# A decoder layer on one core: inputs laid out with the contraction on partitions, cross products first, work spread over PSUM banks and GpSimd

## The reference

```python
x = _layernorm(x + attn(x, q_kernel, k_kernel, v_kernel, out_kernel))   # 16 heads, 4 kv heads, D=128, RoPE, window of 128
x = _layernorm(x + xattn(x, ctx_1024, Wq, bq, Wk, bk))
x = _layernorm(x + ffn(x, ...))                                         # 2 shared + 16 routed experts of width 176, top 4

# xattn(x, ctx, ...)
query = einsum('bnc,dc->bnd', ctx, Wq) + bq
key = einsum('bnc,dc->bnd', ctx, Wk) + bk
attention = softmax(einsum('bnd,bmd->bnm', query, key), axis=-1)
x_m = einsum('bln,bmn->blm', x, attention)
```

## Time and profile before

| what | us |
|---|---|
| median of 3 runs | 410.21 (409.89 to 410.97) |
| the profiled execution, its own time | 410.56 |
| its span, first to last instruction | 408.8 |
| PE busy in the span | 389.0 |
| DVE busy | 284.2 |
| ACT busy | 267.1 |
| POOL busy | 180.1 |

### The profile page before, as it was taken

One profiled execution on the slowest core, in us unless ns is written; L12 is line 12 of the kernel. 1 busy time (PEld: TensorE's weight loads), 2 busy tenths in 40 slices (PEclk: granted clock), 3 DMA queues, 4 the chain that ended last, 5 costly groups with the idle time before them and its releaser, 6 DMA issues.

```text
span 408.8 us, 8464 instructions
## 1 busy us (share of the span) xinstructions
PE 389.0 (95%) x2559; PEld 347.4 (85%) x2559; DVE 284.2 (70%) x796; ACT 267.1 (65%) x670; POOL 180.1 (44%) x314
## 2 busy tenths in 40 slices
PE   6976999999998999999999999999999999999995
PEld 3666898998897999888999878889989998999994
DVE  2785999786786876867787877477659545744445
ACT  3666998776767785866776787565775743444352
POOL 0243766455564743663563675486956300000000
PEclk9996999999999999999999999999999999999999
DMA  6711330000001000000000099322222212243221
GB/s 202 270 53 53 108 124 27 2 2 2 1 2 26 0 0 0 0 0 0 0 0 0 0 261 329 109 79 88 88 85 82 96 59 78 82 152 97 91 64 51
DMA packets 24677, 28.25 MB, mean 69 GB/s; under 512 B 2961, under 2 KB 17194, under 8 KB 24650
## 3 DMA queue, kind: packets, MB, share of 16 engines
q1 hardware_dynamic: 24650, 27.92, 21.6%
HBM read 26.80 MB, written 1.11 MB: 68 GB/s over the span
## 4 chain that ended last, share of the span: by engine, by line
PE 72%; DVE 10%; ACT 7%; issue 5%; POOL 2%; DMA 1%; SPq 1%; DVEq 0%; ACTq 0%; POOLq 0%
PE bank L704 20%; PE bank L706 19%; PE bank L705 19%; PE bank L834 4%; PE bank L843 3%; PE bank L833 2%; PE bank L806 2%; PE bank L800 1%; ACT probs L1091 1%; ACT xln L1100 1%; DVE by_sin L1349 1%; DMA ctx_sb<-in_ctx 1%; DVE pT_lo L1228 1%; DVE by_cos L1348 1%; ACT probs L1089 1%
## 5 line engine op out<-in xcount | busy, mean ns | idle before, releaser
L1022 ACT ACTIVATE hid<-bank,b_cols 128x512 f32<-128x512 f32 x48 | 33.0, 687 | 55.6 <-PE bank L706 47.0
L1245 DVE TENSOR_TENSOR hid<-hid,gate_rows 128x512 f32<-128x512 f32 (+1 forms) x44 | 31.8, 724 | 48.0 <-ACT hid L1022 47.8
L1601 POOL TENSOR_SCALAR nprobs<-probs,rsums 128x128 f32<-128x128 f32 x64 | 24.1, 376 | 76.2 <-DVE rsums L1364 67.8
L705 PE MATMUL bank<-w_lo,hid_hi 128*128 128x256 f32 (+1 forms) x200 | 56.3, 282 | 0.0
L1593 POOL TENSOR_TENSOR queryT<-by_cos,by_sin 128x512 f32<-128x512 f32 x32 | 41.1, 1285 | 26.5 <-DVE by_sin L1349 25.5
L1082 ACT COPY swapped<-bank 64x512 f32<-64x512 f32 x40 | 23.3, 583 | 33.7 <-PE bank L706 33.4
L1228 DVE TENSOR_TENSOR hid_lo<-hid,hid_hi 128x512 fp32r<-128x512 f32 x48 | 36.2, 753 | 5.4 <-ACT hid_hi L1043 5.4
L704 PE MATMUL bank<-xT_hi,wq_hi 128*128 128x256 f32 x128 | 38.4, 300 | 1.4 <-issue 1.2
L705 PEld LDWEIGHTS bank<-w_lo,hid_hi 128*128 128x128 f32 (+1 forms) x200 | 37.7, 188 | 2.1
L706 PE MATMUL bank<-x2T_hi,w_lo 128*128 128x512 f32 (+1 forms) x100 | 39.4, 394 | 0.0
L834 PE MATMUL bank<-keyT,queryT 128*128 128x256 f32 x128 | 38.7, 384 | 0.0
(11 more groups left out here) (177 smaller groups left out, 1239.9 us busy)
## 6 DMA issues: line engine op xcount, KB each, us to landing
gate_rows<-gates_d SPq DMA_DIRECT2D x16, 256.0 KB, 3.1
stage<-in_L_attn_q_kernel SPq DMA_DIRECT2D x4, 512.0 KB, 6.5
stage<-in_L_attn_out_kernel SPq DMA_DIRECT2D x4, 512.0 KB, 3.6
w_raw<-in_L_ffn_routed_w SPq DMA_DIRECT2D x2, 1024.0 KB, 9.5
gate_rows<-gates_d SPq DMA_DIRECT2D x8, 224.0 KB, 3.1
gate_rows<-gates_d SPq DMA_DIRECT2D x8, 192.0 KB, 2.8
gate_rows<-gates_d SPq DMA_DIRECT2D x8, 160.0 KB, 2.5
w_raw<-in_L_ffn_routed_w SPq DMA_DIRECT2D x2, 528.0 KB, 8.0
```

The source lines that it names most:

```text
L705: nc.tensor.matmul(o, sh, ml, start=False, stop=False, **kw)
L1022: nc.scalar.activation(hid[:, u % 2, :], z_bank[u % 3][:], ACT.Relu, bias=b1_cols[:, i % NC:i % NC + 1]).then_inc(relu_done, 1)
L1245: nc.vector.tensor_tensor(own, own, gate_rows[rows, i % 3, :], ALU.mult).then_inc(gated, 1)
L1601: nc.gpsimd.tensor_scalar(nprobs[:, u, 0:W], probs[:, u, 0:W], rsums[:, u, 0:1], 1.0, ALU.mult, ALU.mult)
```

## The change

**Inputs.** `laid_out`, called in `kernel()`, arranges the inputs in DRAM so that the contracted dimension lies on partitions: x transposed for each batch (`xt`), the cross weights, their biases and the context in one array (`cross`), the expert weights with the centroids and the last biases in `w1` and `w2`, the first biases in `small`, the RoPE tables (one head wide) and the mask in one array. The transposes of x, of the context and of the small tensors are gone from PE, with the copies behind them; the loads are fewer and have longer rows.

**x.** The slots x0 and x1 are gone. A new step `x` stands at place -2.5 on ACT (`split_x`: `xT_hi` from the loaded `xraw`, 128x512) and at -2.45 on POOL (`x_low`: `xT_lo`). The q and k slots wait for `x_done`, which POOL gives.

**Once.** The cross products open PE's list, half by half; `E_BANK` and `A_BANK` spread energies and their transposes over banks 4 to 7; the reciprocals of `e_norm` stay on DVE, its multiplications move to POOL, as does the low part of the weight piece q1. `attT` 0 to 3 stand at 1.2, 2.2, 3.3 and 4.2 in place of 1.1, 1.15, 2.1 and 2.15.

```diff
-SLOT_AT = {"x0": -2.5, "x1": -2.5, "q0": -1.25, "k0": -1, ...
+SLOT_AT = {"q0": -1.25, "k0": -1, ...
-    "act": {"slot": 0, "exp": 0.75, ...
+    "act": {"x": -2.5, "slot": 0, "exp": 0.75, ...
-    "pool": {"slot": 0, "normalise": 0.5, ...
+    "pool": {"x": -2.45, "slot": 0, "normalise": 0.5, ...
+POOL_PIECES = ["q1"]
+    "pe": {"cross 0": -2.6, "cross 1": -2.4, "energy 0": -2.3, "energy 1": -2.25, "energy 2": -2.2,
+           "energy 3": -0.7, "attT 0": 1.2, "attT 1": 2.2, "attT 2": 3.3, "attT 3": 4.2},
...
+    "pool": {"e_norm 0": -0.4, "e_norm 1": 0.9, "e_norm 2": 1.9, "e_norm 3": 2.9},
-    E_BANK = [6, 7, 4, 5]
+    E_BANK, A_BANK = [6, 4, 7, 5], [6, 7, 6, 7]
-                if kind == "x":
-                    e.wait_ge(ld_xb, 16 * (b + 1))
-                    for t in range(TT):
-                        mm = nc.tensor.transpose(o[:, t * P:(t + 1) * P], xb[:, t, j * P:(j + 1) * P], ident[:])
-                    e.wait_ge(emptied, slot_count(b, "x1"))
+                    e.wait_ge(x_done, b + 1)
+            def split_x(b, _):
+                e.wait_ge(ld_xt, 16 * (b + 1))
+                if not (isinstance(b, int) and b == 0):
+                    e.wait_ge(projected, NSLOT * b - len(LATE))
+                nc.scalar.copy(xT_hi[:], xraw[:]).then_inc(x_hi_done, 1)
+            def x_low(b, _):
+                e.wait_ge(x_hi_done, b + 1)
+                nc.gpsimd.tensor_tensor(xT_lo[:], xraw[:], xT_hi[:].bitcast(F32), ALU.subtract).then_inc(x_done, 1)
+            def once(work, of):                                        # on POOL
+                if work == "piece":
+                    e.wait_ge(w_hi, of + 1)
+                    nc.gpsimd.tensor_tensor(PIECES[of][2], stage_view(of), PIECES[of][1].bitcast(F32),
+                                            ALU.subtract).then_inc(w_lo_pool, 1)
+                    return
+                c = int(work[-1])
+                e.wait_ge(dve, place("dve", f"e_rsum {c}"))
+                for t in range(TT):
+                    ins = nc.gpsimd.tensor_scalar(e_exp[:, c, t, :], e_exp[:, c, t, :], e_rsum[:, c, t:t + 1], 1.0,
+                                                  ALU.mult, ALU.mult)
+                ins.then_inc(e_normed, 1)
```

More of the change, by code:

```diff
@@ L147, in window_order @@
     turns += [(at, "once", name, 0) for name, at in ONCE_AT[engine].items()]
-    if engine in ("act", "dve"):
-        turns += [(at, "once", "piece", PIECE_NAMES.index(name)) for name, at in PIECE_AT.items()]
+    turns += [(PIECE_AT[name], "once", "piece", PIECE_NAMES.index(name)) for name in PIECES_OF[engine]]
     return [(window, work, of) for _, window, work, of in sorted(turns, key=lambda e: e[0])]
@@ L624, in _ @@
-            row_of = lambda c: first + (c - full - 1) * P
-            def load_w1(g):
-                a, z = W_GROUPS[g][0:2]
-                src, a0 = (s1, 0) if a < NS else (r1, NS)
-                for k in range(KC):
-                    if z == NE:
-                        part_of = w1_raw[:, k, (NE - 1) * FF:TOP * P]
-                        sp.dma_start(part_of, src[:, k, NR - 1, 0:FF - LAST]).then_inc(ld_w[g], 16)
-                    whole = min(z, NE - 1)
-                    sp.dma_start(w1_v[:, k, a:whole], src[:, k, a - a0:whole - a0]).then_inc(ld_w[g], 16)
@@ L850, in values @@
                 e.wait_ge(emptied, slot_count(b, LAST_V))
+                if isinstance(b, int) and b == 0 and g == 0 and blk == 0:
+                    after("act", "attT 2")
                 if not is_last(b, g, blk):
@@ L1128, in once @@
                     piece(of)
-                elif work == "ctx turned":
-                    after("xwT")
-                    step(nc.scalar.copy(xwT[:].rearrange("p a d -> p (a d)"), bank[3][:, 0:2 * D]), "xwT")
-                    after("ctxT 0")
-                    step(nc.scalar.copy(ctxT[:, 0:HALF], bank[6][:]), "ctxT 0")
-                elif work == "ctx projected":
-                    for h in range(2):
-                        after(f"xp 0 {h}")
-                        step(nc.scalar.activation(xqT[:, h * HALF:(h + 1) * HALF], bank[4 + h][:], ACT.Identity,
-                                                  bias=xb_cols[:, 0:1]), f"xqT {h}")
+                elif work[:-2] == "cross":
+                    h = int(work[-1])
+                    after(f"xp 0 {h}")
+                    step(nc.scalar.activation(xqT[:, h * HALF:(h + 1) * HALF], bank[4 + h][:], ACT.Identity,
+                                              bias=xb_cols[:, 0:1]), f"xqT {h}")
                 elif work[:-2] == "e_exp":
@@ L1145, in once @@
                     step(ins, work)
-                elif work == "small turned":
-                    after("smallT")
-                    nc.scalar.copy(centT[:].rearrange("p k r -> p (k r)"), bank[7][:, 0:KC * NR])
-                    step(nc.scalar.copy(b1_cols[:], bank[7][:, 64:64 + NC]), "smallT")
                 else:
@@ L1152, in once @@
                     after(work)
-                    step(nc.scalar.copy(attT[:, c, :, :].rearrange("p k r -> p (k r)"), bank[E_BANK[c]][:]), work)
+                    step(nc.scalar.copy(attT[:, c, :, :].rearrange("p k r -> p (k r)"), bank[A_BANK[c]][:]), work)
             for s in (exp_done, pT_hi_done):
@@ L1692 @@
[L1692 to L1695 removed]
+    "pe": once_order("pe", {f"cross {h}": [f"xp {a} {h}" for a in range(2)] for h in range(2)}),
+    "act": once_order("act", {f"cross {h}": [f"xqT {h}"] for h in range(2)}),
@@ L1702 @@
     nc = bacc.Bacc("TRN2", target_bir_lowering=False, num_devices=1)
-    cos_c, sin_c = rope_tables()
-    consts = {"cos_c": cos_c, "sin_c": sin_c, "mask_c": window_mask(), "ident_c": np.eye(P, dtype=np.float32)}
     arrays, args = {}, []
-    for name, a in [(n, inputs[n]) for n in _INS] + list(consts.items()):
+    for name, a in laid_out(inputs).items():
         a = np.ascontiguousarray(a)
```

313 lines of the change are left out of this document (126 added, 187 removed).

## The result

The changed kernel takes 423.58 us (median of 4 runs, 422.42 to 424.42) against 410.28 before: a ratio of 1.032, 95% interval 1.029 to 1.0351. It is slower, as forecast, and inside the range (412 to 424), near its upper end. Its profiled execution is the fastest of the four, 422.42 us, with a span of 420.4, 11.6 more than before.

What follows compares the result with a forecast made beforehand. PE's list, practically full from 40 us, bounds the kernel. Span 408.8 - 2.0 (first batch) + 7.5 (loop-head stalls) + 3.9 (clock) = 418.2; with 1.76 outside, 420.0 profiled, median 419.6; range 412 to 424.

Steps and rivals of the forecast that it cites:

- The loop head: At three loop heads q0 waits for POOL's xT_lo, PE idling 3.7 us; 3 x 2.5 = 7.5 us lost.
- link 5: Loop head, chain to q0: POOL's xT_lo behind head 13's normalisation, priced at 1.285 us like its add, ending at 130.8.
- The clock: Granted clock falls at the three loop-head idle times, 1.3 us each: 3.9 us lost, at most 7.5.
- Rival A: Loop heads: the same 7.5 us lost to waiting, but the clock stays at 2.4 GHz; 415.7 us, chance 0.33.
- The forecast's middle between 0 and 2.5: Loop heads: price of one clock fall, taken as 1.3 us at each of three places.
- The first batch: Up to about 44 us: PE's new list gains 2.0 us, at best 4.0, lower end 0.
- the long tour: First batch: attT 2 waits for a whole tour over POOL's list, 8 to 9 us after attT 0.
- the signs named beforehand: q0 released by xT_lo after about 3.7 us idle, three times; clock dips; first score near 18.7; head 2 at 39.6 to 42.
- Rival C: Whole kernel: first batch gains 5 to 6, making good 5.7 lost at loop heads; 410.4 us, no difference, chance 0.06.
- Rival B: Loop heads: POOL reaches xT_lo before 126.1, q0 does not wait, each pass gains 0.9; 405.5 us, chance 0.09.
- the lists as printed: Loop head: on ACT x follows oT_hi, ahead of head 13's exponentials; on POOL head 13 stands before x.

Runs made afterwards that it cites:

- x_low_first: Changed kernel with POOL's xT_lo subtraction placed ahead of the normalisation of head 13, not behind it: 412.28 us, 1.0047 of before.
- busy_at_heads: Changed kernel with 13 idle products on PE at each loop head, ahead of its wait for x, filling the idle time: 419.57 us, 1.0226 of before.
- x_next_early: Changed kernel with the split of the next batch's x moved some three places ahead, into the batch before (ACT 12.2, POOL 12.3): 408.31 us, 0.9954 of before.
- busy_in_first: Changed kernel with 13, 15 and 4 idle products on PE ahead of its first-batch waits for attT 0, 2 and 3: 421.29 us, 1.0296 of before.
- q1_piece_on_dve: Changed kernel with weight piece q1 as before the change, cast on ACT and subtracted on DVE at -0.9: 426.92 us, 1.0429 of before.
- early_x_norms_dve: Changed kernel with both the early split of the next x and the e_norm multiplications back on DVE: 401.40 us, 0.9796 of before.
- norms_on_dve: Changed kernel with the four e_norm multiplications back on DVE, right behind their reciprocals, instead of on POOL: 416.73 us, 1.0166 of before.

## Why the prediction was nearly right, and where it was not

**The loop head** is as told. From the end of `oT_hi` to q0 the prediction had 126.6 to 130.9, 4.3 us; the rows have 130.74 to 134.79, 4.05. The nearest row for link 5, POOL's add of 1.285, was the right one: `xT_lo` took 1.26 to 1.27 us. DVE was idle during it at all three heads (its `pT_lo` ends at 133.09 at batch 2), where the prediction had it at work that reads a bank. By the rule of the Trainium skill, page SBUF — State Buffer, section Who interferes with whom, such work would not have disturbed it; the trace of x_low_first agrees, where `xT_lo` began while DVE's `oT_lo` read a bank (127.21 to 127.89) and took 1.27 us. PE idled 3.0 to 3.3 us, not 3.7. The stall cost 6.6 us, forecast 7.5.

**The clock** fell at all three heads, and cost 4.9, forecast 3.9. Rival A, the stall without the fall, is what busy_at_heads made by hand: 419.6, and 417.8 in its profiled run, against A's 415.7 and the first batch's missing 2 us. The forecast's middle between 0 and 2.5 was a choice without a row; the rows now say 1.7, because the low clock began with PE's work, or 0.1 us ahead of it at the third head, and almost nothing of it lay in the idle time. The advice of the Trainium skill, page TensorE: Matmul & The Clock Gate, section Why this matters for your kernels, against long idle gaps between bursts of matmuls was borne out: the clock fell after idle times of 3.0 to 3.3 us and not after the 1.1 to 1.2 us of x_low_first.

Together the heads were forecast at 11.4 us and took 11.5. The closeness of the sum is luck: the stall was 0.9 too dear and the clock 1.0 too cheap. The mechanism of both was right.

**The first batch** is the term that was mis-sized: a gain of 2.0, measured -0.16. In the four other kernels that have the same first batch the slot of `v` lies between 42.97 and 45.15, against 43.97 before. The gain is zero within this spread, and the low clock is part of the spread: the second low stretch lasts 10.2 us in x_next_early and 6.8 in the changed kernel. The steps of the working, with rows of the changed kernel that answer to the earlier trace rows:

```profile
16.06 0.39 PE L645 MATMUL bank<-xT_hi,wq_hi 128*128 128x256 f32 x1 [1.30 <-DVE by_cos L1270]
...
20.33 0.49 PE L770 MATMUL bank<-keyT,queryT 128*128 128x128 f32 x2 [0.29 <-POOL keyT L1503]
...
25.12 0.63 PE L861 MATMUL bank<-ident,e_exp 128*128 128x128 f32 x4 [3.22 <-POOL e_exp L1572]
...
35.97 0.83 PE L861 MATMUL bank<-ident,e_exp 128*128 128x128 f32 x4 [3.70 <-POOL e_exp L1572]
...
39.88 1.09 PE L861 MATMUL bank<-ident,e_exp 128*128 128x128 f32 x4 [1.15 <-POOL e_exp L1572]
...
43.88 0.38 PE L782 MATMUL bank<-ident,nprobs 128*128 128x128 f32 x2
```

| step | forecast | changed | busy_in_first, clock at 1.00 |
|---|---|---|---|
| first score | 18.7 | 20.33 | 20.19 |
| `attT 0` | 23.6 | 25.12 | 24.94 |
| `attT 2` behind `attT 0` | 8 to 9 | 10.85 | 9.58 |
| `attT 3` behind `attT 2` | 3.5 to 4.7 | 3.91 | 3.94 |
| head 2 behind `attT 3` | 2.1 | 4.00 | 2.58 |
| head 2 | 39.6, or 41.7 with the fall | 43.88 | 41.04 |

Of the 2.2 us of error at head 2, 0.7 is the clock (2.8 measured, 2.1 forecast) and 1.4 is there at the upper clock too. Nearly all of this 1.4 was made before `attT 0`. From there to head 2 the forecast's 16.0 us met 16.1 by luck: its own terms, the ranges and 2.1 in the table, add up to 13.6 to 15.8 and not to 16.0, and the long tour took more than its range. In that tour POOL and DVE held each other up (POOL's `nprobs` at 31.66 took 1.13 us instead of 0.37, DVE's `by_sin` at 33.62 1.40 instead of 0.68). ACT, DVE and POOL ahead of the first score:

```profile
12.96 1.05 ACT L929 CAST wq_hi<-stage 128x1024 fp32r<-128x1024 f32 x1 [1.30 <-DMA stage<-in_wq]
14.03 0.58 ACT L1013 COPY swapped<-bank 64x512 f32<-64x512 f32 x1
```

```profile
15.31 0.69 DVE L1270 TENSOR_TENSOR by_cos<-bank,tables 128x512 f32<-128x512 f32 x1 [0.60 <-ACT swapped L1014]
15.92 1.07 DVE L1271 TENSOR_TENSOR by_sin<-swapped,tables 128x512 f32<-128x512 f32 x1
16.92 0.68 DVE L1270 TENSOR_TENSOR by_cos<-bank,tables 128x512 f32<-128x512 f32 x1
17.52 1.39 DVE L1271 TENSOR_TENSOR by_sin<-swapped,tables 128x512 f32<-128x512 f32 x1
```

```profile
14.09 2.36 POOL L1566 TENSOR_TENSOR wq_lo<-stage,wq_hi 128x1024 fp32r<-128x1024 f32 x1 [4.96 <-ACT wq_hi L929]
17.07 1.28 POOL L1503 TENSOR_TENSOR queryT<-by_cos,by_sin 128x512 f32<-128x512 f32 x1 [0.63 <-DVE by_sin L1271]
```

The step that failed here is the start of q1 on PE, which waits for `by_cos` of q0 and came at 16.06. The working put nothing ahead of ACT's two copies of q0. In the rows the cast of the piece q1 stands there: it waited 1.30 us for its load, ended at 14.01, and held the copies up by 0.7 us, since q0's last matmul had ended at 13.32. Another 0.3 is q0 itself (11.62 for 11.3), and 0.3 more its twelve matmuls (1.70 for 1.44); the rest are hand-overs and the 0.29 below. q1_piece_on_dve shows that the cast could not simply be put back.

I had also priced `by_sin` at the 0.69 of `by_cos`. The first three took 1.07, 1.39 and (at 19.61) 1.22 us, each with a POOL instruction running as it began. This looks like the cause of the delay, and I took it for one when I wrote what I expected of q1_piece_on_dve, but it cost little: at the first score PE waited 0.29 us for POOL, having finished its list up to there at 20.04, and the chain to `attT 0` goes from the end of q2 at 20.04 over ACT's copies to a `by_sin` at 22.00 that took 0.71.

Of the signs named beforehand, those of the loop head came true but for the length of the idle time (3.0 to 3.3 us for 3.7), and the two of the first batch did not: the first score near 18.7, and head 2 between 39.6 and 42.

**Rival C** fell with this term. **Rival B** had the right place and the right mechanism: x_next_early is that case, and its 1.0 to 1.3 us a pass are B's 0.9. The forecast said that the lists as printed exclude it, and they did.

**From the span to the median.** 418.2 against 420.4 is the first batch. Outside the span were 2.0 us, not 1.76. The median lies 1.2 above the profiled execution, where I had put it 0.35 below. 2.2 + 0.3 + 1.5 are the 4.0 us between 419.6 and 423.6. The last belongs to the spread of this kernel's runs, which lie 2.0 us apart; those of early_x_norms_dve, whose clock is at 1.00 through the batches, lie 0.5 apart. That the varying length of the low stretches makes this spread is likely, and not shown.

## What to carry to other kernels

When work moves from the engine that is full to one that has time, what counts is the place in the queue: here an operand that was ready 2.2 us earlier stood behind a step with a longer chain of its own, and one position more in POOL's list was worth 11 us of 13. Where an edit brings TensorE an idle time of the size seen here (3.0 to 3.3 us), add the slow work behind it to its price: 4.9 us of clock came on top of 6.6 us of stall. An order that follows the chain of each operand, not the place where it is used, is cheap to try. Here it turned +3.2% into -0.5%, and with the multiplications of `e_norm` back on DVE into -2.0%.

## What the runs showed of the chip that I had not expected

- Idle times of 3.0 to 3.3 us at a loop head stand in four of the kernels (changed, norms_on_dve, busy_in_first, q1_piece_on_dve), twelve in all, and each is followed by a stretch at 0.50. The fall does not come at one point: in the changed kernel it is 1.1 and 0.45 us after PE had started again (72.72 and 73.81, 134.79 and 135.25) and 0.1 us before at the third head; over the twelve it lies between 0.85 us before and 1.1 us after. Eleven of the stretches last 3.4 us and one 6.8. Idle times of 1.09 to 1.19 us at the same place brought no fall.
- Longer idle times brought longer stretches at two of three heads: 4.66 and 4.67 us were followed by 6.8 us at 0.50, but 4.36 us by 3.4.
- A DVE instruction with both inputs in SBUF that begins while POOL computes is not slowed in proportion: it seems to stand until POOL's instruction ends. `by_sin` of 17.52 ends 0.56 us behind the add beside it (18.91 and 18.35), and the one of 22.00, which met only the end of an add, 0.55 us behind that add's end. A piece's subtraction of 128x1024 takes 1.22 us on DVE alone and 2.29 beside an add of POOL (18.15 to 20.44, the add ended at 19.36). `by_cos`, which reads a bank, took 0.68 beside the same kind of add. It goes the other way too: `nprobs` of 128x256 takes 0.48 us on POOL, and 1.44 where it began under DVE's subtraction of a piece (66.73 in the changed kernel).
